# Expert rows added onto the output by adding scatters, in a fused graph layer with a mixture of experts

## What is computed

```python
sel = _route(x, hash_proj, K_ACTIVE)                  # two experts of 64 for each token
buf = jnp.zeros((E, C, d), x.dtype).at[se, posc].add(xr)
h = jax.nn.gelu(jnp.einsum('ecd,edf->ecf', buf, W1), approximate=False)
y = jnp.einsum('ecf,efd->ecd', h, W2)
out = y[se, posc] * keep[:, None].astype(x.dtype)
...
out = expert_outputs.mean(axis=1)
...
x = x + _L0_ffn_ref(_layernorm(x, axis=-1)[None], ...)[0]
```

## Time and profile before

| | us |
|---|---|
| median of 3 runs | 613.05 (612.96 to 616.77) |
| the profiled execution | 614.53 |
| its span | 612.6 |
| busy: PE, DVE, ACT, POOL | 513.3, 327.0, 256.6, 87.9 |
| DMA traffic | 106.07 MB, of it 64 loads of 1 MB |

### The profile page before, as it was taken

One profiled execution on the slowest core, in us unless ns is written; L12 is line 12 of the kernel. 1 busy time (PEld: TensorE's weight loads), 2 busy tenths in 40 slices (PEclk: granted clock), 3 DMA queues, 4 the chain that ended last, 5 costly groups with the idle time before them and its releaser, 6 DMA issues.

```text
span 612.6 us, 8157 instructions
## 1 busy us (share of the span) xinstructions
PE 513.3 (84%) x2674; PEld 352.5 (58%) x2675; DVE 327.0 (53%) x810; ACT 256.6 (42%) x515; POOL 87.9 (14%) x91
## 2 busy tenths in 40 slices
PE   2879999899989999999999999227999977977710
PEld 1334443344679888999999998213545443544400
DVE  5888778688875546488853236970222212122236
ACT  2988887599545322366642224322222211111100
POOL 4001111000000000000000000036444443211110
PEclk9999999799999999999999999757999999899965
DMA  9400000000200049100030029945999999999258
GB/s 313 146 2 1 1 1 1 2 1 2 68 1 1 0 161 398 54 1 2 25 147 1 1 107 425 421 181 155 365 417 415 418 413 417 418 422 401 103 188 335
DMA packets 27656, 106.07 MB, mean 173 GB/s; under 512 B 4907, under 2 KB 5804, under 8 KB 19292
## 3 DMA queue, kind: packets, MB, share of 16 engines
q1 hardware_dynamic: 17372, 86.01, 35.1%
q0 software_dynamic: 5120, 10.26, 4.6%
q10 hardware_dynamic: 5120, 9.26, 4.2%
HBM read 93.41 MB, written 18.63 MB: 183 GB/s over the span
## 4 chain that ended last, share of the span: by engine, by line
PE 64%; SPq 11%; DMA 9%; DVE 9%; issue 3%; ACT 2%; DVEq 1%; POOL 0%; POOLq 0%; ACTq 0%
SPq L1428 10%; PE PS L483 8%; PE PS L482 8%; PE PS L484 7%; PE PS L751 5%; DMA BIG<-in_we 5%; PE PS L557 5%; PE PS L520 5%; PE PS L764 5%; PE PS L586 4%; PE PS L587 4%; PE PS L512 4%; PE PS L698 3%; PE PS L546 2%; DMA BIG<-y_rows 2%
## 5 line engine op out<-in xcount | busy, mean ns | idle before, releaser
L1139 DVE COPY BIG<-PS 128x512 f32<-128x512 f32 x32 | 22.1, 692 | 126.2 <-PE PS L764 126.2
L482 PE MATMUL PS<-ROUND 128*128 128x416 f32 (+3 forms) x232 | 83.8, 361 | 0.0
L483 PE MATMUL PS<-ROUND 128*128 128x416 f32 (+3 forms) x232 | 83.6, 360 | 0.0
L484 PE MATMUL PS<-ROUND 128*128 128x416 f32 (+3 forms) x232 | 83.3, 359 | 0.0
L764 PE MATMUL PS<-BIG 128*64 128x512 f32 x256 | 61.5, 598 | 1.4 <-DVE BIG L1134 1.4
L875 DVE TENSOR_TENSOR BIG<-PS,BIG 128x280 f32 x92 | 41.2, 448 | 22.1 <-PE PS L546 16.3
L1383 POOL DMA_INDIRECT y_rows<-BIG,SCIDX x32 | 32.3, 1010 | 100.4 <-DVE BIG L1139 98.2
L857 DVE TENSOR_SCALAR BIG<-BIG 128x280 f16<-128x280 f16 x157 | 45.6, 325 | 0.0
L586 PE MATMUL PS<-ROUND 128*128 128x416 f32 (+3 forms) x120 | 43.5, 363 | 2.3 <-DVE ROUND L891 1.8
L484 PEld LDWEIGHTS PS<-ROUND 128*128 128x128 f32 (+1 forms) x232 | 43.6, 188 | 2.5
L482 PEld LDWEIGHTS PS<-ROUND 128*128 128x128 f32 (+1 forms) x232 | 43.5, 188 | 2.6
(11 more groups left out here) (221 smaller groups left out, 846.7 us busy)
## 6 DMA issues: line engine op xcount, KB each, us to landing
BIG<-in_we SPq DMA_DIRECT2D x64, 1024.0 KB, 26.4
y_rows<-KVB SPq DMA_DIRECT2D x19, 256.0 KB
BIG<-y_rows SPq DMA_DIRECT2D x9, 512.0 KB, 7.9
BIG<-in_wqkvp ACTq DMA_DIRECT2D x3, 1024.0 KB, 16.4
XA<-in_x SPq DMA_DIRECT2D x9, 256.0 KB, 8.9
out<-BIG ACTq DMA_DIRECT2D x9, 256.0 KB
BIG<-in_w1g SPq DMA_DIRECT2D x1, 2048.0 KB, 8.3
BIG<-in_w2g SPq DMA_DIRECT2D x1, 2048.0 KB, 14.1
```

The lines of the kernel that those rows point to most:

```text
L482: mm(o, ah, bh, start=first, stop=False)
L483: mm(o, ah, bl, start=False, stop=False)
L484: return mm(o, al, bh, start=False, stop=last)
```

## The change

`y_rows`, its clearing, the reload, the sums and the final stores are gone. In their place:

1. Behind each store of normalised rows ScalarE stores the tile of `XA` to the output, ten stores.
2. VectorE halves the result while it copies it out of the bank.
3. Per pair GpSimd issues two indirect DMAs onto the output that add (`compute_op=ALU.add`): the rows for which this expert is the lower of the token's two (`IDX1`), and those for which it is the higher (`IDX2`); for either, the other rows' indices are out of bounds. The second add of a pair waits until the first add of the same pair has landed, and is issued behind the first add of the next pair. `LATER` (two comparisons on VectorE) says which choice is the higher; five small operations on VectorE make the two tables.
4. `XA` isn't needed once it is stored. Its first eight tiles become two more weight buffers, `NR` = 18. Their first loads wait for the stores of four tiles each.
5. The wait for weights counts per pair of experts, not per expert; the general loop is changed in the same way.

```diff
-        YL = big(6024, 10240).rearrange("p (i a d) -> p i a d", i=NT, a=2)
-        yv = y_d.rearrange("(t a) d -> t a d", a=2)
...
+        ring += [XA[:, 4 * q:4 * q + 4, :].rearrange("p i d -> p (i d)") for q in range(2)]
         NR = len(ring)
...
-            for sm, value in stored(sd_ys, 31, NY):
+            for sm, value in stored(sd_y1, 31, NY) + stored(sd_y2, 31, NY):
                 eng.wait_ge(sm, value)
...
-                    for j in range(2):
-                        e = 2 * r + j
-                        pe.wait_ge(sd_we[e % NR], 16 * (e // NR + 1))
+                    pe.wait_ge(sd_we[r % (NR // 2)], 32 * (2 * r // NR + 1))
...
+                later = LATER.rearrange("p (i k) -> p i k", i=NT)
+                V.tensor_tensor(later[:, :, 0:1], pairs[:, :, 0:1], pairs[:, :, 1:2], ALU.is_gt)
+                V.tensor_tensor(later[:, :, 1:2], pairs[:, :, 1:2], pairs[:, :, 0:1], ALU.is_ge).then_inc(s_sel, 1)
...
-            V.scalar_tensor_tensor(SCIDX[:, :], PS[:, b, 0:32], -1.0, VIDX[:, 1, :], ALU.add, ALU.add).then_inc(moved[b], 1)
+            V.scalar_tensor_tensor(IDS[:, :], PS[:, b, 0:32], -2.0, VIDX[:, 1, :], ALU.add, ALU.add).then_inc(moved[b], 1)
             dve.wait_ge(moved[b], use)
-            V.tensor_scalar(TIDX[:, :], SCIDX[:, :], 1, None, ALU.arith_shift_right).then_inc(s_tidx, 1)
+            V.tensor_scalar(TIDX[:, :], IDS[:, :], 1, None, ALU.arith_shift_right).then_inc(s_tidx, 1)
+            link(V.tensor_scalar(ODDS, IDS[:, :], 1, None, ALU.bitwise_and))
+            dve.wait_ge(s_tidx, 1)
+            V.scalar_tensor_tensor(IDX1, ODDS, 4096.0, TIDX[:, :], ALU.mult, ALU.add).then_inc(s_tidx, 1)
+            link(V.tensor_scalar(IDX2, TIDX[:, :], 4096.0, None, ALU.add))
+            V.scalar_tensor_tensor(IDX2, ODDS, -4096.0, IDX2, ALU.mult, ALU.add).then_inc(s_tidx, 1)
...
-                        dve.wait_ge(sd_ys[r % NY], 16 * (r // NY))
-                    V.tensor_copy(YS[r % NY], PS[:, b, :]).then_inc(moved[b], 1)
+                        dve.wait_ge(sd_y1[r % NY], 16 * (r // NY))
+                        dve.wait_ge(sd_y2[r % NY], 16 * (r // NY))
+                    V.tensor_scalar(YS[r % NY], PS[:, b, :], 0.5, None, ALU.mult).then_inc(moved[b], 1)
...
-            for i in range(NT):
-                n = rows(i)
-                dve.wait_ge(sd_row[i], 32)
-                link(V.tensor_tensor(YL[0:n, i, 0, :], YL[0:n, i, 0, :], YL[0:n, i, 1, :], ALU.add))
-                V.scalar_tensor_tensor(YL[0:n, i, 0, :], YL[0:n, i, 0, :], 0.5, XA[0:n, i, :], ALU.mult,
-                                       ALU.add).then_inc(s_res, 1)
...
                     act.dma_start(xx_d[128 * i:128 * i + n, :], XX[i % 4][0:n, :]).then_inc(sd_xxs[i % 4], 16)
+                    act.dma_start(out[128 * i:128 * i + n, :], XA[0:n, i, :]).then_inc(sd_base[i // 4], 16)
...
-            for i in range(NT):
-                n = rows(i)
-                act.wait_ge(s_res, 1 + i + 1)
-                act.dma_start(out[128 * i:128 * i + n, :], YL[0:n, i, 0, :]).then_inc(sd_out, 16)
...
+            def add_rows(r, idx, done):
+                G.indirect_dma_start(out=out[:, :], out_offset=bass.IndirectOffsetOnAxis(ap=idx[:, r:r + 1], axis=0),
+                                     in_=YS[r % NY], in_offset=None, compute_op=ALU.add, bounds_check=N - 1,
+                                     oob_is_err=False).then_inc(done[r % NY], 16)
+
+            def first_rows(r):
+
                 b, use = at_of(("down", r))
                 pool.wait_ge(moved[b], use)
...
+                add_rows(r, IDX1, sd_y1)
+
+            def second_rows(r):
+
+                pool.wait_ge(sd_y1[r % NY], 16 * (r // NY + 1))
+                add_rows(r, IDX2, sd_y2)
...
             for r in range(32):
                 if r + NX < 32:
                     b, use = at_of(("tr", r))
                     pool.wait_ge(full[b], use)
                     gather_pair(r + NX)
                 if r != 1:
-                    scatter_pair(max(r - 1, 0))
-            scatter_pair(31)
+                    q = max(r - 1, 0)
+                    first_rows(q)
+                    if q:
+                        second_rows(q - 1)
+            first_rows(31)
+            second_rows(30)
+            second_rows(31)
...
-            sp.wait_ge(s_pool, 5)
-            for i in range(20):
-                n = min(128, 2 * N - 128 * i)
-                sp.dma_start(y_d[128 * i:128 * i + n, :], ZERO[0:n, :]).then_inc(sd_yz, 16)
...
-            for e in range(2, NR):
+            for e in range(2, NR - 2):
                 load_expert(e)
+            for g in range(2):
+                sp.wait_ge(s_nrm2, 4 * g + 4)
+                sp.wait_ge(sd_base[g], 16 * 4)
+                load_expert(NR - 2 + g)
...
-            for i in range(NT):
-                n = rows(i)
-                sp.dma_start(YL[0:n, i, :, :], yv[128 * i:128 * i + n, :, :]).then_inc(sd_row[i], 16)
```

More of the change, by code:

```diff
@@ L398, in gnn_mix_moe @@
         VIDX = RT[:, 4200:4264].rearrange("p (a r) -> p a r", a=2)
+        IDX1, IDX2, ODDS = (scr(32).bitcast(I32) for _ in range(3))
         RT5 = [RT[:, q:q + D] for q in range(0, 4608, D)]
@@ L425, in gnn_mix_moe @@
         sd_row = [sem(f"d_row{i}") for i in range(NT)]
-        sd_edg, sd_cst, sd_vec, sd_brow, sd_w1, sd_hp, sd_w2, sd_yz, sd_out = (
-            sem("d_" + n) for n in ("edg", "cst", "vec", "brow", "w1", "hp", "w2", "yz", "out"))
+        sd_edg, sd_cst, sd_vec, sd_brow, sd_w1, sd_hp, sd_w2 = (
+            sem("d_" + n) for n in ("edg", "cst", "vec", "brow", "w1", "hp", "w2"))
         sd_w = {n: sem("d_w" + n) for n in "kvqp"}
         sd_xxs = [sem(f"d_xxs{q}") for q in range(4)]
-        sd_we = [sem(f"d_we{q}") for q in range(NR)]
+        sd_we = [sem(f"d_we{q}") for q in range(NR // 2)]
         sd_xg = [sem(f"d_xg{q}") for q in range(NX)]
-        sd_ys = [sem(f"d_ys{q}") for q in range(NY)]
+        sd_base = [sem(f"d_base{g}") for g in range(3)]
+        sd_y1 = [sem(f"d_y1{q}") for q in range(NY)]
+        sd_y2 = [sem(f"d_y2{q}") for q in range(NY)]
         (s_pool, s_key, s_dif, s_oh, s_soa, s_sod, s_koh, s_st, s_sq, s_rr, s_xn, s_xh, s_xl, s_res0, s_kr, s_ke,
@@ L455, in gnn_mix_moe @@
         S2 = big(26576, NEXP)[0:M2, :].bitcast(I32)
-        IT, IS = big(26640, 1)[0:M2, :].bitcast(I32), big(26641, 1)[0:M2, :].bitcast(I32)
+        IT, IF, IS = (big(26640 + q, 1)[0:M2, :].bitcast(I32) for q in range(3))
+        F2, O2 = (big(26704 + NEXP * q, NEXP)[0:M2, :].bitcast(I32) for q in range(2))
         DSTC, SRCC = EDG[:, 1, :], EDG[:, 0, :]
@@ L1392, in chain @@
                 pool.wait_ge(s_par, step[0])
-            pool.wait_ge(s_sel, 4)
+            pool.wait_ge(s_sel, 5)
+            chain(G.tensor_tensor(ALO, ALO, LATER, ALU.add))
+            chain(G.tensor_tensor(AIDX, AID, LATER, ALU.add))
             chain(G.tensor_copy(ODD, ODDI))
@@ L1409, in gpsimd @@
                 gather_pair(r)
-            b, use = at_of("slots")
-            pool.wait_ge(moved[b], use)
-            pool.wait_ge(sd_yz, 16 * 20)
+            pool.wait_ge(s_tidx, 3)
+            for g, (a, e) in enumerate(GROUPS):
+                pool.wait_ge(sd_base[g], 16 * (e - a))
             for r in range(32):
@@ L1573, in full_dve @@
             link(V.tensor_copy(V2, PS[0:M2, 0, 0:NEXP]))
-            link(V.tensor_scalar(V3, V2, 1.0, -1.0, ALU.max, ALU.add))
+            link(V.tensor_scalar(V3, V2, 2.0, -2.0, ALU.max, ALU.add))
             link(V.tensor_copy(T2, V3))
@@ L1577, in full_dve @@
             link(V.tensor_scalar(V3, V2, 0.5, 8192.0, ALU.is_lt, ALU.mult))
-            link(V.scalar_tensor_tensor(V3, V2, -1.0, V3, ALU.add, ALU.add))
+            link(V.scalar_tensor_tensor(V3, V2, -2.0, V3, ALU.add, ALU.add))
             link(V.tensor_copy(S2, V3))
+            link(V.tensor_scalar(O2, S2, 1, None, ALU.bitwise_and))
+            link(V.tensor_scalar(S2, S2, 1, None, ALU.arith_shift_right))
+            link(V.scalar_tensor_tensor(F2, O2, 4096.0, S2, ALU.mult, ALU.add))
+            link(V.tensor_scalar(S2, S2, 4096.0, None, ALU.add))
+            link(V.scalar_tensor_tensor(S2, O2, -4096.0, S2, ALU.mult, ALU.add))
             eng.sem_clear(fu["dve"])
@@ L1602, in full_pool @@
                 take(eng, "yc", 1)
-                G.indirect_dma_start(out=y_d[:, :], out_offset=bass.IndirectOffsetOnAxis(ap=IS, axis=0),
-                                     in_=YS[0][0:M2, :], in_offset=None, bounds_check=2 * N - 1,
-                                     oob_is_err=False).then_inc(fu["ys"], 16)
+                for idx in (IF, IS):
+                    G.indirect_dma_start(out=out[:, :], out_offset=bass.IndirectOffsetOnAxis(ap=idx, axis=0),
+                                         in_=YS[0][0:M2, :], in_offset=None, compute_op=ALU.add, bounds_check=N - 1,
+                                         oob_is_err=False).then_inc(fu["ys"], 16)
+                    eng.drain()
                 eng.drain().then_inc(fu["sc"], 1)
```

(1 more changed line is left out.)

32 lines of the change are left out of this document (11 added, 21 removed).

## The result

| | before | after |
|---|---|---|
| median (range), us | 613.0 (610.1 to 616.8) | 645.07 (643.74 to 649.11) |
| ratio after/before | | 1.053, 95% interval 1.046 to 1.061 |
| profiled execution, span | 614.53, 612.6 | 643.74, 641.9 |
| busy: PE, POOL | 513.3, 87.9 | 528.2, 156.6 |

What follows compares the result with a forecast made beforehand. The weight load stream and a 35.6 us tail after it were taken to set the end. 612.6 - 18.9 - 5.1 + 4 + 10 = 602.6 us of span, 603 on the median's scale; range 591 to 625.

Steps and rivals of the forecast that it cites:

- GpSimd's new order: GpSimd's issues per pair, second add waiting for the first: 5.6 us a pair, hidden behind the load stream, 0 us.
- L: Time from an add's issue to its landing, in GpSimd's chain; taken as 7.8 us, a gather's median.
- Rival B: GpSimd's wait for the first add's landing before the second becomes the bound; kernel slower, 622 us; chance 0.18.
- rival A: Adds cost next to nothing in the DMA engines, 0 to 3 us; time 593, or 589; chance 0.2.
- Adds in the engines: DMA engines, adds in place of scatters: reading 4.64 MB of output rows in the busy stretch costs 10 us.
- Two more buffers: Weight loads: two more move into the free stretch before 428, gain 5.1 us as long as loads set the pace.
- The front: Before the experts: copies of x delay normalisation, routing and gathers; experts start 4 us later, bounds 0 and 7.
- The tail: After TensorE's last release at 577.0: 35.6 us become 16.7 without reload and sums, gain 18.9, bounds 20.3 and 12.
- the signs to look for: Signs of a wrong forecast: GpSimd idle until first adds land, VectorE waiting for result buffers, load stream gap before 560.

Runs made afterwards that it cites:

- experiment 2: Changed kernel with each second add issued one pair later, behind the first add two pairs on; 637.85 us, ratio 1.039.
- experiment 5: Changed kernel with each weight load issued as two DMAs of 4 KB per partition in place of 8 KB; 623.55 us, ratio 1.018.
- experiment 1: Changed kernel with both adds per pair as plain scatters that overwrite (compute_op left out), same waits and order; 605.97 us, ratio 0.988.
- experiment 4: Changed kernel with 16 weight buffers again, no loads into XA; 644.26 us, ratio 1.050.
- experiment 3: Changed kernel with the ten copies of x into the output issued together behind the last store of normalised rows; 644.65 us, ratio 1.052.
- experiment 7: Changed kernel without its second adds and their waits, so rows of each token's higher expert are left out; 598.49 us, ratio 0.975.
- experiment 6: Changed kernel with the bounds check of both adds set to 0, so nearly every row is left out; 625.59 us, ratio 1.017.

## Why the prediction was wrong

**The step that failed is "GpSimd's new order", priced at 0, whose cover was called thin.** The formula of that step (two pairs take L, 0.8 from the landing to the next issue, one add and one gather) holds: with an L of 12.3, the mean of the three from 462.16 to 494.63, and the measured 1.86 and 1.39 from issue to issue in place of twice 1.33, it is 12.3 + 0.8 + 1.86 + 1.39 = 16.35 for two pairs, 8.2 a pair, measured 8.15. What failed is L, put at 7.8, a gather's. Landings of gathers were read as times that a transfer takes. Experiments 2 and 5 show the landings of adds as times in a queue: 12.4 us became 19.7 when the awaited add was a pair older, and 7.7 when the packets of the loads were halved. At 0.35 us a packet the 10 packets an engine and pair of before are 3.5 us, under the 4.4 to 5.1 us that the loads give a pair; 23 are 8.1 us. On this path the prediction had the first add of pair 21 at 550.2 and the last at 590.5. They are at 589.1 and 626.3: 20 pairs at 7.4 us in place of 5.6, and then ten at 3.72, two issues of 1.86 end to end, where it had six at 4.95 and four at 2.65. The step followed latency where throughput decided, and the packets that would have told, 5,120 for 64 DMAs and 17,372 for 86 MB, stood in the earlier trace rows. What they could not tell is the 144 of an adding DMA; at 80 each the pair would have had 15 packets and 5.3 us, still over the 4.4 and 5.1 of the loads, and the plain run shows that as 60 us of waits in VectorE. There, with landings of 7.5 to 8.5 us, the L of 7.8 was right; it is the adding form that the step had wrong.

**Rival B** named the place, and its first condition (dearer issues, 1.5 us) came true at 1.55. Its mechanism, the wait, was the cause only until the queue had filled (experiment 2), and its price, 622, was 23 us too low, since L didn't stop at 9.5. Its 6.95 us a pair count the dearer issue twice (the formula gives 6.7), and its 3.15 for the last pairs count it once (two such adds are 3.66, measured 3.72); the two slips nearly cancel. A third has no bearing: in rival A the order of GpSimd alone, by its own formula, ends near 579, not 584.

**Adds in the engines**, put at 10 (bounds 0 and 11.2): the rows' share is 19.5 us on the end, above the upper bound. In engine time, q0 took 54.6 us against 28.2, 26 more, where the price by bytes had 11.2 for the whole of the added reads.

**Two more buffers**, put at -5.1 "as long as loads set the pace": they don't, and it is 0 (experiment 4).

**The front**, put at 4 within 0 to 7, came to 6.85: the first gather is at 418.14, 411.29 before. The mechanism is as told. The wait of the sixth tile, 2.27 us in the earlier trace rows, is 5.66:

```profile
401.49 0.81 ACT L1313 ACTIVATE XG<-XA,NM,RR 128x512 f32<-128x512 f32 x1 [5.66 <-DMA xx_rows<-XG]
```

The last row store is issued 3.4 us later than before (407.12 in the earlier trace rows), and it takes 6.5 us to land, by the chain of waits, where it took at most 4.2 (down by 411.3):

```profile
410.54 6.53 DMA xx_rows<-XG
```

The copies and the two loads into `XA` share its engines; the loads' part in the whole delay is 3.9 us (experiment 4). What it cost at the end is not shown: experiments 3 and 4 took back only 2 us of it at the third pair's add, and their medians moved by 0.4 and 0.8 us.

**The tail**, put at 16.7 us from the last load's release, of which 8.3 until the last first add is issued. VectorE, waiting for buffers until 585, starts its last copies 4.4 us and less apart, while GpSimd works off ten pairs from 589 on at 1.86 us an add (timelines of the two):

```profile
608.25 0.69 DVE L1147 TENSOR_SCALAR BIG<-PS 128x512 f32<-128x512 f32 x1 [3.38 <-PE PS L763]
612.65 0.69 DVE L1147 TENSOR_SCALAR BIG<-PS 128x512 f32<-128x512 f32 x1 [3.38 <-PE PS L763]
...
619.75 0.69 DVE L1147 TENSOR_SCALAR BIG<-PS 128x512 f32<-128x512 f32 x1 [2.12 <-PE PS L763]
```

```profile
589.08 1.58 POOL L1374 DMA_INDIRECT out<-BIG  x1 [0.31 <-issue]
...
626.30 1.55 POOL L1374 DMA_INDIRECT out<-BIG  x1 [0.30 <-issue]
...
630.02 1.55 POOL L1374 DMA_INDIRECT out<-BIG  x1 [0.31 <-issue]
```

The last first add is issued at 626.30, 6.55 us after the start of VectorE's last copy, where the last scatter came 1.5 us behind it (583.86 in the earlier trace rows, 585.33 in the earlier trace rows): 5 us of arrears. From there to the span's end are 15.6 us, where the forecast had 16.7 - 8.3 = 8.4, and 5.9 of that difference of 7.2 weren't in the sum at all. At the end of the program GpSimd has a drain, and all others wait for it. First the change, then the kernel before (duration three times in ns, start in us):

```profile
L243 POOLq DRAIN  x1: 5909/5909/5909, 635.8 to 635.8; - x1
```

```profile
L244 POOLq DRAIN  x1: 5385/5385/5385, 589.1 to 589.1; - x1
```

Before, the same drain ran from 589.1 beneath the reload and the sums and cost nothing. The reload and the sums were its cover, and the change took it away. Experiments 1 and 7 have it at 7.9 and 5.3 us. The drain is also the largest known part of what lies between the plain run (span 604.7) and the sum without adds, 612.6 - 18.9 - 5.1 + 4 = 592.6: 7.9 of 12.1 us. The first gather came 2.9 us later than the 4 in that sum; whether the two buffers gave their 5.1 us there was not tried.

**Right** were the signs to look for, on their wrong side: idle time before the second adds that their own landing ends, VectorE waiting for result buffers, and a load rate that falls before 560 (330 GB/s from 520). The account of the 32 us: experiment 1 is 7.5 under before; the form of the adds gives 20, their rows 19.5. That they split so is shown by leaving out one at a time; as they bind on one another, the split need not hold in another order.

What stays open: how the 20 us of the form divide between packets and dearer issues, what the late front cost, and why an added row costs 2.4 to 2.9 and not 2 times as much as other rows.

## What to carry to other kernels

Before a queue of small indirect DMAs is given more work beside a stream of big ones, count its packets per round, from the page's DMA queues, and multiply by the time of one packet of the stream; if that is over the round's time, expect the queue to be the bound. An older wait gave back 7 of the 32 us here, halved packets in the stream 21.5. The add into memory in place of a reload and a sum moved work to the queue that had least to spare, though its bytes were the same 10.3 MB. And what the removed end was hiding, here GpSimd's drain of 5 to 8 us, belongs in the sum of the tail.

## What was not expected of the hardware

- An indirect DMA of 128 rows of 2 KB has 80 packets as a gather or a plain scatter and 144 as an adding one, as many when nearly all its rows are out of bounds (experiment 6).
- Beside a stream with packets of 8 KB GpSimd's queue got one packet through each engine in 0.31 to 0.38 us; with packets of 4 KB the pair fell from 8.15 us to 5.1 and 6.5 in turn, and 5.1 is its issues end to end.
- An adding DMA of GpSimd's landed 12.4 us after its issue in the full queue, 19.7 when one more pair was issued ahead of the wait, and 7.7 beside packets of 4 KB.
- GpSimd took 1.55 us to issue an adding DMA, 1.0 for a plain one.
- With loads in rows of 8, 4 and 2 KB all DMA traffic ran at 387, 371 and 359 GB/s (440 to 480) beside the same adds.
- GpSimd's drain at the end of the program took 5.3 to 7.9 us.
